# A gated recurrence with a binarised feed-forward block on one core: the orders of work in the opening stage and at the end are changed

## The reference, cut to what matters

```python
def attn(x, W_in, b_in, W_gate, b_gate, A, Bm, C, D, W_out, b_out):   # x: 2 x 4096 x 256
    u = x @ W_in + b_in                      # 64 states
    g = sigmoid(x @ W_gate + b_gate)
    def step(h_prev, (u_t, g_t, x_t)):
        h_t = tanh(h_prev @ A + u_t @ Bm)
        y_t = h_t @ C.T + u_t @ D.T
        return h_t, g_t * y_t + (1 - g_t) * x_t
    ys = scan(step, 0, over the 4096 time steps)
    return ys @ W_out + b_out + x

def ffn(x, w1, b1, w2, b2):                  # w1: 1024 x 256, w2: 256 x 1024
    h = gelu(x @ binarize(w1).T + b1)        # binarize: sign times the row's mean absolute value
    return h @ binarize(w2).T + b2

x = layernorm(x + attn(x, ...))
x = layernorm(x + ffn(x, ...))
```

## Time and profile before

| | before |
|---|---|
| time, median of 3 runs | 431.89 us (431.27 to 434.48) |
| the profiled execution | 431.89 us, of which the span 430.1 us |
| PE busy | 410.3 us, 95% of the span |
| DVE busy | 369.4 us, 86% |
| ACT busy | 321.6 us, 75% |
| POOL busy | 305.8 us, 71% |
| mean granted TensorE clock | 0.986 |

### The profile page before, as it was taken

The page is one execution under the profiler, slowest core; times in us unless marked ns, Lnnn a source line. Parts: engine busy times, 40 slices in busy tenths (PEclk is TensorE's granted clock), DMA queues, the critical chain, the costliest instruction groups (busy, mean ns, idle before and its releaser), DMA issues.

```text
span 430.1 us, 7765 instructions
## 1 busy us (share of the span) xinstructions
PE 410.3 (95%) x2699; PEld 305.9 (71%) x2699; DVE 369.4 (86%) x778; ACT 321.6 (75%) x604; POOL 305.8 (71%) x322
## 2 busy tenths in 40 slices
PE   7999999999949999999999999999999999999992
PEld 5899988788426768677776767768677776766651
DVE  2798889875365999999999999999999999998685
ACT  2257766555546777989898898988989898797981
POOL 6476674336478969797887979779797887683424
PEclk9999999999978999999999999999999999999997
DMA  7954530001100022314225231332413225130322
GB/s 226 368 185 149 170 76 2 1 2 50 51 0 25 25 64 63 72 50 99 96 52 142 56 99 50 98 115 67 115 49 99 100 50 143 54 100 23 77 98 99
DMA packets 43896, 37.19 MB, mean 86 GB/s; under 512 B 35504, under 2 KB 37296, under 8 KB 43856
## 3 DMA queue, kind: packets, MB, share of 16 engines
q1 hardware_dynamic: 42528, 35.66, 29.1%
q0 software_dynamic: 272, 0.66, 0.5%
q10 hardware_dynamic: 1056, 0.36, 0.3%
HBM read 19.90 MB, written 8.39 MB: 66 GB/s over the span
## 4 chain that ended last, share of the span: by engine, by line
PE 67%; DVE 23%; issue 5%; ACT 3%; POOL 1%; DVEq 0%; POOLq 0%; ACTq 0%
PE bank L1089 17%; PE bank L1077 15%; PE bank L938 10%; PE bank L906 7%; DVE hid L1446 7%; PE bank L855 5%; PE bank L917 3%; PE bank L831 3%; DVE gT L1459 3%; DVE bank L1431 3%; PE bank L848 3%; ACT hid L700 3%; DVE bank L1452 2%; DVE gT L1441 2%; PE bank L839 1%
## 5 line engine op out<-in xcount | busy, mean ns | idle before, releaser
L1077 PE MATMUL bank<-xT,w1s 128*128 128x512 f16 x512 | 128.6, 384 | 1.3 <-DVE hid L1446 0.5
L1089 PE MATMUL bank<-w2s,hid 128*128 128x256 f16 x1024 | 125.4, 273 | 1.4 <-DVE hid L1446 0.8
L1089 PEld LDWEIGHTS bank<-w2s,hid 128*128 128x128 f16 x1024 | 98.5, 98 | 32.2 <-issue 4.3
L692 ACT ACTIVATE bank<-bank,b_col,alpha 128x512 f32<-128x512 f32 x128 | 96.7, 756 | 21.9 <-PE bank L1077 21.8
L1446 DVE SCALAR_TENSOR_TENSOR hid<-bank,small,hid 128x512 f16<-128x512 f32 x128 | 95.1, 744 | 12.7 <-ACT hid L700 12.7
L700 ACT ACTIVATE hid<-bank,small 128x512 f16<-128x512 f32 x128 | 86.4, 691 | 18.1 <-PE bank L1089 16.9
L1077 PEld LDWEIGHTS bank<-xT,w1s 128*128 128x128 f16 x512 | 46.5, 99 | 48.3 <-DVE hid L1446 6.3
L639 ACT ACTIVATE hu<-bank 64x128 f32<-64x128 f32 x103 | 27.8, 270 | 44.5 <-PE bank L855 41.8
L453 POOL TENSOR_TENSOR ys_lo<-gT,ys_hi 128x512 fp32r<-128x512 f32 x30 | 38.2, 1277 | 24.8 <-ACT ys_hi L665 24.8
L448 POOL TENSOR_TENSOR gT<-gT,xT 128x512 f32<-128x512 f32 x30 | 38.2, 1274 | 12.9 <-DVE gT L1329 12.8
L469 POOL TENSOR_TENSOR gT<-x_rows,b_row 128x1024 f32<-128x1024 f32 x16 | 38.0, 2377 | 7.7 <-DMA xT<-gT 7.7
(11 more groups left out here) (159 smaller groups left out, 822.2 us busy)
## 6 DMA issues: line engine op xcount, KB each, us to landing
x_load<-in_L_attn_x SPq DMA_DIRECT2D x16, 512.0 KB, 3.4
gT<-in_L_attn_x SPq DMA_DIRECT2D x15, 512.0 KB, 3.7
out_rows<-gT SPq DMA_DIRECT2D x15, 512.0 KB, 3.5
gT<-in_L_ffn_w SPq DMA_DIRECT2D x2, 1024.0 KB, 7.3
gT<-in_L_attn_x SPq DMA_DIRECT2D x4, 128.0 KB, 2.8
out_rows<-gT SPq DMA_DIRECT2D x2, 256.0 KB, 2.2
xT<-gT SPq DMA_TRANSPOSE x28, 3.2
w_gate<-in_L_attn_W_gate ACTq DMA_DIRECT2D x1, 256.0 KB, 7.4
```

The lines of the kernel that those rows point to most:

```text
L692: nc.scalar.activation(bank[which][:, :], bank[which][:, :], ACT.Gelu, bias=b1_col[:, c:c + 1], scale=alpha1[:, c:c + 1]).then_inc(s_gelu, 1)
L1077: done = nc.tensor.matmul(bank[which][:, :], w1s[:, c, k, :], x1T[:, n, :, part, :, k, :], start=(k == 0 and part == 0), stop=(k == KD - 1 ...
L1089: done = nc.tensor.matmul(bank[tile // 2][:, tile % 2 * DM:(tile % 2 + 1) * DM], hid[:, c % 3, part, tile * P:(tile + 1) * P], w2s[:, :, c ...
```

## The change

It changes orders and due times, no computation: in the opening stage the transposes of x come a step later (`turned_at`), the constants' preparation a block of steps later (PREP), and the first y products at steps 86 and 90 instead of 83 and 85 (FIRST_Y); DVE's and POOL's queues are put in another order around them, the loop over the blocks of x among them; at the end of the second stage the queues of PE, ACT and DVE are reordered.

```diff
--- before.py
+++ after.py
@@ -60,12 +60,12 @@
     N = STEPS * P
     T0 = L - WARM
     B0 = T0 // STEPS
-    PREP = 9
+    PREP = 10
     WHOLE_U = 3
     BEFORE = 5
     IN_PARTS = NB - 2
     GATE_ORDER = (9, 12, 15, 2, 5, 0, 1, 6, 7, 8, 3, 4, 10, 11, 13, 14)
-    FIRST_Y = (WARM + 10 * STEPS + 3, WARM + 11 * STEPS + 1)
+    FIRST_Y = (WARM + 11 * STEPS + 2, WARM + 12 * STEPS + 2)
     FIRST_OUT = WARM + L - 7
     assert NS == 64 and KD == 2 and L % STEPS == 0 and T0 % STEPS == 0 and N == 512 and HC == 8
     assert B0 % 2 == 0 and NB % 2 == 0 and sorted(GATE_ORDER) == list(range(NB))
@@ -73,13 +73,13 @@
 
     def turned_at(t):
 
-        return divmod(t + 2 * STEPS + 1, STEPS)
+        return divmod(t + 2 * STEPS, STEPS)
 
     def pieces_at(t):
 
         if t < WHOLE_U * STEPS or t in FIRST_Y or FIRST_OUT <= t < FIRST_OUT + STEPS:
             return 0
-        return 1 if t < NB * STEPS - 7 else 2 if t < NB * STEPS - STEPS else 3
+        return 1 if turned_at(t)[0] < NB + 1 and t < NB * STEPS - 7 else 2 if t < NB * STEPS - STEPS else 3
 
     def pieces_before(t):
         return sum(pieces_at(i) for i in range(t))
@@ -519,12 +519,12 @@
                     pool.tensor_tensor(xg_lo[:, 0, k, :], xT[:, GATE_ORDER[place], k, :], xg_hi[:, 0, k, :].bitcast(F32),
                                        ALU.subtract).then_inc(s_xgl[0], 1)
 
-            gate_x_low(6)
-            pool.wait_ge(s_xgl[0], 2)
+            for place in (6, 8, 10):
+                gate_x_low(place)
+            pool.wait_ge(s_xgl[0], 6)
             hu_low(0, 0)
             hu_low(0, 1)
-            for place in (8, 10, 12):
-                gate_x_low(place)
+            gate_x_low(12)
             ys_low(0, 0)
             ys_low(0, 1)
             pool.wait_ge(s_const, 3)
@@ -797,18 +797,19 @@
             for c in (6, 7):
                 hidden_gelu(NB - 2, c)
                 hidden_hi(NB - 2, c)
-            hidden_gelu(NB - 1, 0)
+            for c in range(2):
+                hidden_gelu(NB - 1, c)
+                hidden_hi(NB - 1, c)
+            hidden_gelu(NB - 1, 2)
             second_norm(NB - 4, 1)
-            hidden_hi(NB - 1, 0)
-            hidden_gelu(NB - 1, 1)
-            second_norm(NB - 4, 2)
-            hidden_hi(NB - 1, 1)
-            hidden_gelu(NB - 1, 2)
             hidden_hi(NB - 1, 2)
             hidden_gelu(NB - 1, 3)
-            hidden_hi(NB - 1, 3)
+            second_norm(NB - 4, 2)
+            hidden_gelu(NB - 1, 4)
             second_norm(NB - 4, 3)
-            for c in range(4, HC):
+            for c in range(3, 5):
+                hidden_hi(NB - 1, c)
+            for c in range(5, HC):
                 hidden_gelu(NB - 1, c)
                 hidden_hi(NB - 1, c)
             act.wait_ge(s_last_shift, 1)
@@ -963,7 +964,7 @@
                     done.then_inc(s_a2p, 1)
                     pe.wait_ge(s_prep, 4)
                     nc.tensor.transpose(bank[4][0:1, 0:P], bound_max, ident[:, :]).then_inc(s_mt, 1)
-                if s == 3:
+                if s == 2:
                     pe.wait_ge(s_m1, 1)
                     nc.tensor.matmul(bank[5][:, 0:1], ones[0:1, :], bound_all, start=True,
                                      stop=True).then_inc(s_mb, 1)
@@ -995,7 +996,6 @@
                     transpose_step(3, 3)
                 if t == 7:
                     u_whole(2, 1)
-                    transpose_step(*turned_at(t))
 
             for t in range(WARM + L):
                 o, s = divmod(t, STEPS)
@@ -1009,8 +1009,8 @@
                     if t == 2 * STEPS:
                         pe.wait_ge(s_wp, 2)
                     u_part(o + 1, s // 2, s % 2)
-                    if turned_at(t)[0] < NB:
-                        transpose_step(*turned_at(t))
+                    if o + 2 < NB:
+                        transpose_step(o + 2, s)
                 if t == WHOLE_U * STEPS:
                     pe.wait_ge(s_wgs, 2)
                 for i in range(pieces_before(t), pieces_before(t + 1)):
@@ -1160,10 +1160,10 @@
                 iteration(n)
 
 
+            hidden(NB - 1, 0)
             ffn_out(NB - 2, 5)
-            hidden(NB - 1, 0)
+            hidden(NB - 1, 1)
             ffn_out(NB - 2, 6)
-            hidden(NB - 1, 1)
             ffn_out(NB - 2, 7)
             hidden(NB - 1, 2)
             hidden(NB - 1, 3)
@@ -1238,39 +1238,27 @@
             x_out(3, 1)
             u_out(2, 1)
             x_high(3, 1)
-            x_out(4, 0)
-            u_out(3, 0)
-            x_high(4, 0)
-            for o in range(WHOLE_U, NB - 1):
-                x_out(o + 1, 1)
-                u_out(o, 1)
-                x_high(o + 1, 1)
+            for o in range(2, NB - 1):
+                if o >= WHOLE_U:
+                    u_out(o, 1)
+                    x_out(o + 1, 1)
+                    x_high(o + 1, 1)
                 if o + 2 < NB:
                     x_out(o + 2, 0)
                 u_out(o + 1, 0)
                 if o + 2 < NB:
                     x_high(o + 2, 0)
             gate_x_hi(5)
+            u_out(NB - 1, 1)
             gate_x_lo(5)
-            u_out(NB - 1, 1)
+
 
             dve.wait_ge(s_w12, 32)
             nc.vector.tensor_reduce(alpha1[:, :], w1_stage, AX.X, ALU.add, apply_absolute_value=True)
             gate_x_hi(6)
             nc.vector.tensor_reduce(alpha2[:, :], w2_stage, AX.X, ALU.add, apply_absolute_value=True).then_inc(s_prep, 1)
-
-            def first_y_high(half):
-
-                dve.wait_ge(s_h, 1 + WARM + STEPS)
-                dve.wait_ge(s_sgn, 2)
-                nc.vector.tensor_copy(y0_hu_hi[HALVES[half], :, :], beside(0, half)).then_inc(s_huhi, 1)
-
-            dve.wait_ge(s_prep, 1)
-            first_y_high(0)
-            first_y_high(1)
             gate_x_hi(7)
             gate_x_lo(7)
-            gate_x_hi(8)
             dve.wait_ge(s_prep, 1)
 
             dve.wait_ge(s_wc, 96)
@@ -1280,6 +1268,7 @@
                                     ALU.subtract).then_inc(s_wsplit, 1)
             dve.wait_ge(s_wsplit, 2)
             nc.vector.memset(ones, 1.0)
+            gate_x_hi(8)
             dve.wait_ge(s_const, 3)
             for k in range(KD):
                 nc.vector.tensor_scalar(diag[:, k, :], ident[:, :], alpha2[:, k:k + 1], 1.0 / H, ALU.mult,
@@ -1295,6 +1284,8 @@
             nc.vector.tensor_scalar(alpha1[:, :], alpha1[:, :], 1.0 / (DM * X_SCALE), None, ALU.mult).then_inc(s_prep, 1)
 
             gate_x_hi(9)
+            gate_x_lo(9)
+            gate_x_hi(10)
             nc.vector.tensor_scalar(half_b_out[:, :], half_b_out[:, :], 0.5, None, ALU.mult).then_inc(s_hb, 1)
             dve.wait_ge(s_cdp, 1)
             nc.vector.tensor_copy(cd_hi[:, :], bank[2][:, 0:DM]).then_inc(s_cd, 1)
@@ -1303,8 +1294,16 @@
 
             dve.wait_ge(s_mt, 1)
             nc.vector.tensor_reduce(bound_all, bank[4][0:1, 0:P], AX.X, ALU.max).then_inc(s_m1, 1)
-            gate_x_lo(9)
-            gate_x_hi(10)
+            def first_y_high(half):
+
+                dve.wait_ge(s_h, 1 + WARM + STEPS)
+                dve.wait_ge(s_sgn, 2)
+                nc.vector.tensor_copy(y0_hu_hi[HALVES[half], :, :], beside(0, half)).then_inc(s_huhi, 1)
+
+            gate_x_hi(11)
+            first_y_high(0)
+            first_y_high(1)
+            gate_x_lo(11)
             dve.wait_ge(s_mb, 1)
             nc.vector.tensor_scalar(bound_pow, bank[5][:, 0:1], 2.0 ** -100, None, ALU.max).then_inc(s_prep, 1)
             dve.wait_ge(s_prep, 6)
@@ -1316,8 +1315,7 @@
             nc.vector.reciprocal(hid_scale, inv_scale).then_inc(s_prep, 1)
             dve.wait_ge(s_a2p, 1)
             nc.vector.tensor_scalar(alpha2_row[:, :], bank[3][:, 0:DM], inv_scale, None, ALU.mult).then_inc(s_prep, 1)
-            gate_x_hi(11)
-            gate_x_lo(11)
+            gate_x_hi(12)
 
             def less_x(n, m):
                 dve.wait_ge(s_ymm, n * KD + m + 1)
@@ -1344,16 +1342,15 @@
                 nc.vector.tensor_copy(y0_hi[:, m, :], y0_stage[:, m, :]).then_inc(s_yhi, 1)
 
             less_x(0, 0)
+            gate_x_hi(13)
+            first_gate(0)
+            gate_x_lo(13)
+            first_mix(0)
             less_x(0, 1)
-            first_gate(0)
             first_gate(1)
-            first_mix(0)
-            gate_x_hi(12)
+            first_high(0)
             first_mix(1)
-            first_high(0)
             first_high(1)
-            gate_x_hi(13)
-            gate_x_lo(13)
 
             dve.wait_ge(s_h, 1 + WARM + L)
             nc.vector.tensor_tensor(gap, end_state, guess, ALU.subtract).then_inc(s_cmp, 1)
@@ -1571,11 +1568,11 @@
             second_moments(NB - 3)
             hidden_lo(NB - 2, 7)
             hidden_lo(NB - 1, 0)
-            ffn_scale(NB - 2, 0)
             hidden_lo(NB - 1, 1)
-            second_sum(NB - 2, 0)
-            ffn_scale(NB - 2, 1)
-            second_sum(NB - 2, 1)
+            for pair in range(2):
+                ffn_scale(NB - 2, pair)
```

(4 more changed lines are left out.)

## The result

| | before | after |
|---|---|---|
| time, median | 431.81 us (431.27 to 434.48) | 444.82 us (444.19 to 445.14) |
| the profiled execution, its span | 431.89, 430.1 us | 445.74, 443.9 us |
| PE, DVE, ACT, POOL busy | 410.3, 369.4, 321.6, 305.8 us | 416.0, 365.7, 321.9, 304.9 us |

The ratio is 1.0287, with a 95% interval of 1.0243 to 1.0331. The forecast was 447.1 us, its range 441.5 to 449.5. DVE and POOL are busy for less time than before: instructions that had run beside one another are shorter (gate_x_hi 0.79 us in the mean instead of 0.92, gate_x_lo on DVE 1.42 instead of 1.58, first_high 0.70 instead of 1.32). What was added is waiting.

The account below looks back on a forecast made before the run. It took PE, full in both stages with next to no slack per scan step, to bound the kernel. Terms 5.3 - 0.95 + 1.95 + 4.4 + 1.3 + 0.5 = 12.5, with the clock 15.2: 431.9 + 15.2 = 447.1 us, range 441.5 to 449.5.

Parts of the forecast that it names:

- the ring: x loop: low u product, u_out, x_out, POOL's low part and back take 4.07 us against 3.66; +5.3 us.
- place 7: Gate place 7 in the opening stage: PE's wait for DVE's low part goes; -0.95 us.
- step 86: First y product: PE waits for DVE's and POOL's work queued from gate_x_hi(11) on; +1.95 us.
- step 97: First out products: PE waits for ys_low, since hi(13) now stands ahead of DVE's work for them; +4.4 us.
- the first half of the end: Last blocks of the second stage: reordered queues delay the second pair of ffn_out(15,0); +1.3 us.
- The fall of the clock: Steps 98 to 103: PE's idle wait halves its clock for about 5.4 us; +2.7 us.
- the last scaling's delay: Very end: last_moments(1) behind shift2 makes POOL's second root and the last scaling late; +0.5 us.
- The gate piece at step 58: x loop's end: the gate piece of place 4 must pass ahead of the last low product; 0.48 us.
- the ring with slack: Rival, x loop: legs overlap and nothing is paid before step 60; 441.8 us, chance 0.08.
- The later transposes: Opening stage: transposes of x a step later cost 0, bounds -0.2 and +0.3 us.
- a shared rate: Step 86, alternative to DVE and POOL alternating: gate_x_lo(11) ends 0.8 us later, whole sum 13.3 instead of 12.5.
- The other side: Rival, steps 60 to 96: relieving DVE and POOL of each other decides; 430.9 us, chance 0.05.

Follow-up runs that it names:

- experiment 2: The kernel before, with only u_out(o,1) put ahead of x_out(o+1,1) in DVE's x loop: 436.32 us, 4.9 above before.
- experiment 1: The changed kernel, with DVE copying x_out(o+1,1) ahead of u_out(o,1) again: 442.82 us, ratio to before 1.0255.
- experiment 9: The kernel before, with only the transposes of x a step later: 434.51 us beside 431.53, ratio 1.0063.
- experiment 10: The kernel before, with both first_y_high behind gate_x_lo(7) instead of ahead of gate_x_hi(7): 431.98 us beside 431.53.
- experiment 6: The changed kernel, with both first_y_high and the chain ending in alpha2_row ahead of gate_x_hi(11): 443.2 us, 1.6 below the changed kernel's.
- experiment 3: The changed kernel, with gate_x_hi(13) and gate_x_lo(13) behind both halves' less_x, gate, mix and high, as before: 439.43 us, 5.4 below the changed kernel's.
- experiment 4: The changed kernel, with 14 products that nobody reads issued by PE ahead of the wait at step 97: 443.26 us, 1.6 below the changed kernel's.
- experiment 8: The kernel before, with only shift2 put ahead of last_moments(1): 431.61 us beside 431.96, ratio 0.9994.
- experiment 11: The kernel before, with 6 and 14 unread products in PE's two long waits at the second stage's start: 429.94 us, ratio 0.9961.

## Why the prediction was right, point by point

The time lay in the range, and the ring, place 7, step 86, step 97 and the first half of the end were where they had been put, each within 0.3 us. The fall of the clock was mis-sized, the last scaling's delay had next to no effect, and two terms came out right by luck in part. The sum was 15.2 us, and the trace gives 13.1 apart from the later begin; over half of the difference is the clock.

- *The ring*: +5.3 predicted, +5.03 measured. The legs were right to 0.02 us each; the mean turn was 4.04 instead of 4.065. The gate piece at step 58 did come ahead of the low product (69.82 and 70.30). Its rival, the ring with slack, is refuted by experiment 2. One bound was added up wrong: 12 turns at 0.35 us and the gate piece's 0.48 make about +4.6, not +4.4. So was the range's upper end, 449.3 and not 449.5.
- *The later transposes "cost nothing"*: right for this sum, but only because the longer ring hides what they cost; this was luck, since the prediction had not looked for a second ring. I compared x_out's release with u_out's instead of closing the ring through the transposes: 0.34 + 0.42 + 0.72 + 0.52 + 0.51 + 1.34 = 3.85 (the rows of experiment 1). Alone they cost 3.0 us (experiment 9), ten times the bound of +0.3; beside the new order they took some 0.7 us away (experiment 2), more than the bound of -0.2.
- *Place 7*: -0.95 predicted and measured. Experiment 10 shows that the move of DVE's instructions alone gains nothing; it takes more of the change, by the time lines the new order of POOL's queue, which I had not counted as a condition. So this hit is partly luck.
- *Step 86*: +1.95 predicted, +1.78 measured; DVE and POOL finished 0.09 us apart. DVE and POOL took turns, as the sum assumed: the low part took 2.19 us beside POOL instead of 1.23, where a shared rate, by the prediction's estimate of 0.8 us more, would have made it 3.0. Experiment 6 shows that DVE's order is the cause.
- *Step 97*: +4.4 predicted, 4.1 measured; experiment 3 shows that DVE's order is the cause, the clock's fall included: with it undone, 5.4 of the 5.65 us go.
- *The clock*: the mis-sized term. The fall came, and I took 5.4 us at half speed from the one fall in the middle of the trace. It lasted 3.4 us, nearly all of it after the wait, and cost 1.56 us (1.6 by experiment 4) instead of 2.7. But the size differs from execution to execution: in experiment 1's, with the same wait, 5.5 us at half speed came after the wait, and steps 97 to 103 took 0.9 us longer still, a cost of about 2.5. What decides between the two is not shown.
- *The end*: +1.3 predicted, 1.56 measured up to ffn_out(15,0). shift2's +0.5 was wrong in its result: the scaling is 0.45 us late, but the spans show about 0.1, since the last store lands sooner (experiment 8). I had followed the chain to the last instruction and not to the last byte.
- *The other side*: DVE and POOL out of each other's way at place 7 were worth just the 0.95 us there, and could not decide, since the ring did not fit (4.04 us against 3.66).

## What to carry to other kernels

Where a loop runs over several queues, close each ring of waits through it with start-to-start distances and compare it with the beat; a swap of two lines that look independent can lengthen a ring that had only 0.3 us of slack, and a second ring just behind it stays hidden until the first is mended. Ahead of a due step, count all that an engine's queue must still do once its last blocking wait ends. A wait of PE costs more than its length when the clock falls in it, and products that nobody reads can save that: 1.6 us at step 97 (experiment 4) and 1.6 us at the start of the second stage (experiment 11).

## What was not expected of the hardware

The clock was at half speed for 3.4 us in one execution and for 6.8 us in another with the same wait of 3.9 us (the changed kernel and experiment 1); in the second it fell 1.3 us before the wait's end, in the first 0.2 us after it. With the last two stores of 256 KB issued 0.39 us apart the span ended 2.74 us after the second one's issue, with 0.85 us between them 2.40 us (the kernel before and experiment 8).
